# Second attention of a two-layer transformer kernel: values weighed in fp32 as two 64-column tiles, and the output projected inside the loop of head pairs

## What is computed

```python
xn = layernorm(x, ln_x_g, ln_x_b)              # the context, 77 rows
ln = layernorm(latents, ln_l_g, ln_l_b)        # the tokens, 1024 rows
q = heads(ln @ Wq)                             # 16 heads of 64
k, v = heads(concatenate([xn @ Wkv, ln @ Wkv]))
qn = rmsnorm(q, qn_g) * scale
kn = rmsnorm(k, kn_g)
attn = softmax(masked(qn @ kn.T))              # 1024 queries, 1024 + 77 keys
out = (attn @ v).reshape(1024, 16 * 64)
return out @ Wout + bout                       # added to the residual
```

## Time and profile before

| | us |
|---|---|
| median of 3 runs | 2465.91 |
| lowest and highest run | 2465.64, 2475.62 |
| profiled execution, span | 2477.3 |
| loop of pairs (736 to 1935 us of the span), PE busy | 1157.4 of 1199.0 |
| stage that projects the outputs (1942 to 2023 us), PE busy | 71.9 of 81.0 |

### The profile page before, as it was taken

The page is one execution under the profiler, slowest core; times in us unless marked ns, Lnnn a source line. Parts: engine busy times, 40 slices in busy tenths (PEclk is TensorE's granted clock), DMA queues, the critical chain, the costliest instruction groups (busy, mean ns, idle before and its releaser), DMA issues. The chain is left out here.

```text
span 2477.3 us, 40299 instructions
## 1 busy us (share of the span) xinstructions
PE 2096.9 (85%) x13062; PEld 1762.3 (71%) x13063; DVE 1409.2 (57%) x3260; ACT 1135.1 (46%) x2179; POOL 764.3 (31%) x733
## 2 busy tenths in 40 slices
PE   5889539997159999999999999999998863799994
PEld 3569535664149988899998898988898753466772
DVE  4370236664638777777778877778877314321223
ACT  3443202221127667666677766666766311222220
POOL 2100002332164443454444444434541000122220
PEclk9898759999569999999999999999999985899997
DMA  5421351111200000000000000000000347111113
GB/s 192 142 85 55 142 190 37 44 47 41 81 20 1 16 17 16 2 16 16 16 16 16 1 16 17 16 17 1 16 10 9 106 152 263 41 34 31 32 34 113
DMA packets 85352, 131.30 MB, mean 53 GB/s; under 512 B 9825, under 2 KB 70943, under 8 KB 83115
## 3 DMA queue, kind: packets, MB, share of 16 engines
q1 hardware_dynamic: 74539, 106.16, 12.6%
q0 software_dynamic: 8320, 20.65, 2.9%
q10 hardware_dynamic: 2304, 2.10, 0.2%
HBM read 87.89 MB, written 40.80 MB: 52 GB/s over the span
## 5 line engine op out<-in xcount | busy, mean ns | idle before, releaser
L1585 ACT ACTIVATE a_probT<-a_slot 128x512 fp32r<-128x512 f32 (+1 forms) x512 | 320.4, 651 | 345.6 <-PE a_slot L1480 343.5
L1639 DVE TENSOR_REDUCE a_part_peak<-a_slot 128x1 f32<-128x512 f32 (+1 forms) x512 | 354.6, 731 | 154.4 <-PE a_slot L1471 150.0
L1686 DVE TENSOR_TENSOR a_probT<-a_slot,a_probT 128x512 fp32r<-128x512 f32 (+1 forms) x512 | 369.6, 753 | 18.2 <-ACT a_probT L1585 15.6
L1471 PE MATMUL a_slot<-a_KHL,a_QHL 128*128 128x512 f32 (+1 forms) x1536 | 337.2, 355 | 20.9 <-DVE a_probT L1686 14.4
L1494 PE MATMUL a_po<-a_probT,a_VHL 128*128 128x256 f32 (+1 forms) x2322 | 339.9, 291 | 11.1 <-DVE a_O L1705 4.4
L1471 PEld LDWEIGHTS a_slot<-a_KHL,a_QHL 128*128 128x128 f32 x1536 | 271.9, 190 | 94.9 <-DVE a_probT L1686 37.9
L1494 PEld LDWEIGHTS a_po<-a_probT,a_VHL 128*128 128x128 f32 (+1 forms) x2322 | 293.2, 189 | 24.6 <-issue 24.6
L1480 PE MATMUL a_slot<-ident,a_prob 128*128 128x128 f32 x2048 | 282.9, 282 | 10.6 <-issue 10.2
L1577 ACT ACTIVATE a_prob<-a_slot,a_npeak 128x1024 f32<-128x1024 f32 x256 | 284.6, 1112 | 1.0 <-DVE a_npeak L1641 1.0
L1480 PEld LDWEIGHTS a_slot<-ident,a_prob 128*128 128x128 f32 x2048 | 221.7, 142 | 11.3 <-issue 10.7
L1420 PE MATMUL a_side<-a_W,a_latT 128*128 128x128 f32 x1536 | 194.7, 281 | 14.1 <-DMA a_W<-in_L_xattn_Wkv_dram 9.6
(11 more groups left out here) (331 smaller groups left out, 3411.3 us busy)
## 6 DMA issues: line engine op xcount, KB each, us to landing
m_up<-_L_ffn_gate_up_proj_dram SPq DMA_DIRECT2D x8, 1024.0 KB
a_o_rows<-a_O SPq DMA_DIRECT2D x16, 512.0 KB, 3.5
a1o_o<-a_o_rows SPq DMA_DIRECT2D x16, 512.0 KB, 3.5
m_up<-in_L_ffn_W_dram SPq DMA_DIRECT2D x8, 1024.0 KB
m_down<-in_L_ffn_W_dram SPq DMA_DIRECT2D x8, 1024.0 KB
a_prob_dram<-a0p_zeros SPq DMA_DIRECT2D x4, 1632.0 KB, 10.6
a_dist_dram<-a_dist SPq DMA_DIRECT2D x4, 1632.0 KB, 8.2
a_band_prob<-a_prob_dram SPq DMA_DIRECT2D x4, 1632.0 KB, 7.0
```

The lines of the kernel that those rows point to most:

```text
L1471: ins = t_.matmul(out[:, lo:hi], q, KHL[:, pair.parity, h, part, lo:hi], start=part == 0, stop=part == 1)
L1585: a_.activation(probT[:, u // 2 % 2, 0, lo:hi, u % 2, :], slot[u % 2][:, lo * P:hi * P].rearrange("p (t q) -> p t q", q=P), ACT.Copy).then ...
L1639: v.tensor_reduce(part[:, i:i + 1], slot[u % 2][:, lo:hi], AX.X, ALU.max).then_inc(part_peaked, 1)
L1686: v.tensor_tensor(pT[:, 1], slot[u % 2][:, lo * P:hi * P].rearrange("p (t q) -> p t q", q=P), pT[:, 0], ALU.subtract).then_inc(probT_low, 1)
```

## The change

- **Values and probabilities** are plain fp32, without a high and a low part. `V` holds 64 columns a head. `probT` is copied once: the first 4 tiles by ACT (`copy_first`), the other 5 by DVE (`copy_rest`), each as soon as its half is turned.
- **Groups** are four units: both heads, 256 queries. For each of the 9 key tiles `weigh` issues one fp32 matmul for each head, with 64 stationary columns and 256 moving ones: head 0 writes PSUM partitions 0 to 63, head 1 partitions 64 to 127. The 9 tiles are spread over four units as 2, 2, 2 and 3 (`PARTS`). `weigh` now stands ahead of `piece` in PE's order. `fold_outputs` is gone.
- **Sums**: `invert` also widens the inverses to 64 columns a head (`rwide`), PE transposes them into `side` (`turn_sums`, unit 2 of 4), ACT copies them (`copy_sums`), and `normalise` multiplies the transposed outputs by them (unit 0 of 4).
- **Output projection**: in unit 1 of 4, `project_outputs` multiplies the two 128-query tiles with the pair's 128 rows of `Wout` into `side` (two fp32 matmuls of 256 columns), and DVE adds all 512 columns to `xres` (`add_outputs`). `bout` is added to `xres` once, by POOL, after its first pair (`based`), and DVE waits for it ahead of its first unit. The later stage is gone, and so are the stores to HBM and the loads from it.
- `side` is now shared: PE waits for `added` and `r_out` ahead of the piece of such a unit, and for the copy of the piece before ahead of `project_outputs` and `turn_sums`.
- The three weight transfers of a pair are one, from an array laid out by pair on the host. Four memsets of POOL go. `all_pairs` writes out the first and the last pair and loops over the six between.

```diff
+PARTS = [[8, 0], [1, 2], [3, 4], [5, 6, 7]]
...
+def group_before(pair, u, by):
+
+    gi = u // 4 - by
+    return (pair, gi) if gi >= 0 else (pair.previous(), gi + GROUPS)
...
-        probT = sb("probT", [P, 2, 2, KT_TILES, 2, P], F32R)
+        probT = sb("probT", [P, 2, KT_TILES, 2, 2 * P])
...
+            pool.wait_ge(w_out_loaded, 32)
+            g_.tensor_tensor(xres[:, :, :], xres[:, :, :], bout[:, :].unsqueeze(1).to_broadcast([P, TILES, E]),
+                             ALU.add).then_inc(based, 1)
             body(Pair(1, 0, 0, 1), False)
...
                 if part == 0:
-                    pe.wait_ge(probT_low, (pair.g * GROUPS + gi) * 4 + 5)
-                    pe.wait_ge(o_out, pair.g * GROUPS + (gi + 2))
+                    pe.wait_ge(probT_act, pair.g * UNITS + (gi + 1) * 4)
+                    pe.wait_ge(probT_dve, pair.g * UNITS + (gi + 1) * 4)
+                    if gi or not (isinstance(pair.g, int) and pair.g == 0):
+                        pe.wait_ge(normalised, pair.g * GROUPS + gi)
                     if gi == 0:
-                        pe.wait_ge(dve_freed, count(pair, "Vb", SPLIT))
-                for j in range(KT_TILES):
+                        pe.wait_ge(act_freed, count(pair, "Vb", COPIED))
+                for j in PARTS[part]:
                     rows = P if j < S else CTX
-                    ins = t_.matmul(po_t, VHL[0:rows, pair.parity, j, gi % 2, :, :].rearrange("p a d -> p (a d)"),
-                                    probT[0:rows, gi % 2, part, j, :, :].rearrange("p t q -> p (t q)"),
-                                    start=part == 0 and j == 0, stop=part == 1 and j == S)
-                if part == 1:
+                    for h in range(2):
+                        ins = t_.matmul(po_t[h * D1:(h + 1) * D1, :], V[0:rows, pair.parity, j, h, :], probT[0:rows, gi % 2, j, h, :],
+                                        start=j == PARTS[0][0], stop=j == PARTS[-1][-1])
+                if part == len(PARTS) - 1:
                     ins.then_inc(weighed, 1)
 
-            def fold_outputs(pair, gi):
-
-                pe.wait_ge(OT_out, pair.g * GROUPS + (gi + 3))
-                for i in range(2):
-                    ins = t_.matmul(po_n[:, i * D1:(i + 1) * D1], OT[:, i * P:(i + 1) * P], fold[:, :], start=True, stop=True)
-                ins.then_inc(folded, 1)
+            def turn_sums(pair, gi):
+
+                pe.wait_ge(widened, pair.g * GROUPS + (gi + 1))
+                for t in range(2):
+                    ins = t_.transpose(side[:, t * P:(t + 1) * P],
+                                       rwide[:, t, :, :].rearrange("p h d -> p (h d)"), ident[:, :])
+                ins.then_inc(r_turned, 1)
+
+            def project_outputs(pair, gi):
+
+                pe.wait_ge(normalised, pair.g * GROUPS + (gi + 1))
+                for t in range(2):
+                    ins = t_.matmul(side[:, t * E:(t + 1) * E], OT[:, t * P:(t + 1) * P],
+                                    Wout[:, bass.ds(pair.hp, 1), :].rearrange("p a n -> p (a n)"), start=True, stop=True)
+                ins.then_inc(y_done, 1)
...
+                    one_before, two_before = group_before(pair, u, 1), group_before(pair, u, 2)
                     turn(pair, u)
-                    if u % 2 == 0:
-                        fold_outputs(*(pair, u // 2 - 2) if u >= 4 else (before, u // 2 - 2 + GROUPS))
+                    if u % 4 == 1 and two_before[0]:
+                        owner, gi = two_before
+                        if after:
+                            pe.wait_ge(act_freed if PIECES[u - 1] in COPIED else dve_freed,
+                                       count(after, PIECES[u - 1], COPIED if PIECES[u - 1] in COPIED else SPLIT))
+                        else:
+                            pe.wait_ge(r_out, owner.g * GROUPS + (gi + 1))
+                        project_outputs(owner, gi)
+                    if u % 4 == 2 and one_before[0]:
+                        owner, gi = one_before
+                        if after:
+                            pe.wait_ge(act_freed if PIECES[u - 1] in COPIED else dve_freed,
+                                       count(after, PIECES[u - 1], COPIED if PIECES[u - 1] in COPIED else SPLIT))
+                        elif two_before[0]:
+                            pe.wait_ge(added, owner.g * GROUPS + gi)
+                        turn_sums(owner, gi)
+                    if one_before[0]:
+                        weigh(*one_before, u % 4)
                     if after:
+                        if u % 4 == 1 and two_before[0]:
+                            pe.wait_ge(added, two_before[0].g * GROUPS + (two_before[1] + 1))
+                        if u % 4 == 2 and one_before[0]:
+                            pe.wait_ge(r_out, one_before[0].g * GROUPS + (one_before[1] + 1))
                         piece(after, PIECES[u])
-                    weigh(*(pair, u // 2 - 1) if u >= 2 else (before, GROUPS - 1), u % 2)
                     nxt = ahead(pair, u, 2)
                     if nxt[0]:
-                        pe.wait_ge(probT_low, (pair.g * UNITS + u) * 2 + 3)
+                        pe.wait_ge(probT_act, pair.g * UNITS + (u + 1))
+                        pe.wait_ge(probT_dve, pair.g * UNITS + (u + 1))
                         score(*nxt)
...
+            def copy_first(pair, u):
+
+                act.wait_ge(turned, (pair.g * UNITS + u) * 2 + 1)
+                t, h = tile_head(u)
+                a_.activation(probT[:, u // 4 % 2, 0:HALF, h, u % 2 * P:(u % 2 + 1) * P],
+                              slot[u % 2][:, 0:HALF * P].rearrange("p (t q) -> p t q", q=P), ACT.Copy).then_inc(probT_act, 1)
+
+            def copy_sums(pair, gi):
+
+                act.wait_ge(r_turned, pair.g * GROUPS + (gi + 1))
+                a_.activation(rT[:, :], side[:, 0:2 * P], ACT.Copy).then_inc(r_out, 1)
...
-                        copy_outputs(*(pair, u // 2 - 1) if u >= 2 else (before, GROUPS - 1))
...
+            def copy_rest(pair, u):
+
+                dve.wait_ge(turned, (pair.g * UNITS + u) * 2 + 2)
+                t, h = tile_head(u)
+                v.tensor_copy(probT[:, u // 4 % 2, HALF:KT_TILES, h, u % 2 * P:(u % 2 + 1) * P],
+                              slot[u % 2][:, HALF * P:KT_TILES * P].rearrange("p (t q) -> p t q", q=P)).then_inc(probT_dve, 1)
+
...
-                r = rsum[:, gi % 4, :]
-                dve.wait_ge(row_summed, (pair.g * GROUPS + gi) * 2 + 7)
-                v.reciprocal(r, r).then_inc(rsum_done, 1)
+                r = rsum[:, gi % 2, :, :]
+                dve.wait_ge(row_summed, (pair.g * GROUPS + (gi + 1)) * 4)
+                v.reciprocal(r, r).then_inc(inverted, 1)
+                dve.wait_ge(inverted, pair.g * GROUPS + (gi + 1))
+                v.tensor_copy(rwide[:, :, :, :], r.unsqueeze(3).to_broadcast([P, 2, 2, D1])).then_inc(widened, 1)
 
             def normalise(pair, gi):
 
-                n = pair.g * GROUPS + (gi + 3)
-                r = rsum[:, gi % 4, :]
-                dve.wait_ge(rsum_done, n)
-                dve.wait_ge(folded, n)
-                if gi == 0:
-
-                    dve.wait_ge(o_stored[pair.parity], (pair.g - pair.parity) * 8 + 16)
-                t, h = tile_head(2 * gi)
-                v.tensor_tensor(O[:, pair.parity, t:t + 2, h * D1:(h + 1) * D1], po_n.rearrange("p (t d) -> p t d", t=2),
-                                r.unsqueeze(2).to_broadcast([P, 2, D1]), ALU.mult).then_inc(o_out, 1)
+                dve.wait_ge(r_out, pair.g * GROUPS + (gi + 1))
+                dve.wait_ge(weighed, pair.g * GROUPS + (gi + 1))
+                v.tensor_tensor(OT[:, :], po_t, rT[:, :], ALU.mult).then_inc(normalised, 1)
+
+            def add_outputs(pair, gi):
+
+                dve.wait_ge(y_done, pair.g * GROUPS + (gi + 1))
+                tile = pair.b * S + 2 * gi
+                x = xres[:, tile:tile + 2, :].rearrange("p t e -> p (t e)")
+                v.tensor_tensor(x, x, side[:, :], ALU.add).then_inc(added, 1)
...
-                    if u % 2 == 0:
-                        normalise(*(pair, u // 2 - 2) if u >= 4 else (before, u // 2 - 2 + GROUPS))
-                    copy_low(pair, u, 0)
-                    copy_low(pair, u, 1)
+                    two_before = group_before(pair, u, 2)
+                    if u % 4 == 0 and two_before[0]:
+                        normalise(*two_before)
+                    copy_rest(pair, u)
+                    if u % 4 == 1 and two_before[0]:
+                        add_outputs(*two_before)
                     row_sum(pair, u)
-                    if u % 2:
-                        invert(*(pair, u // 2 - 1) if u >= 2 else (before, GROUPS - 1))
+                    if u % 4 == 3:
+                        invert(pair, u // 4)
...
-        with ExitStack() as c3:
...
```

More of the change, by code:

```diff
@@ L1364, in body @@
                     tiles = nat.shape[1]
-                    if j == 0:
-                        pool.wait_ge(high, count(pair, step, SPLIT))
```

(44 more changed lines are left out.)

169 lines of the change are left out of this document (38 added, 131 removed).

## The result

| | before | after |
|---|---|---|
| median of 4 runs each, us | 2466.82 | 2485.56 |
| lowest and highest run, us | 2465.64, 2475.62 | 2483.53, 2486.92 |
| profiled execution, span, us | 2477.3 | 2481.7 |
| from the first turn to the end of the phase, us | 735.59 to 2022.20: 1286.6 | 724.38 to 2026.78: 1302.4 |
| plain pair (median, from one piece c to the next), us | 74.3 | 80.5 |

The ratio is 1.0064, with a 95% interval of 1.0045 to 1.0083: the change makes the kernel slower, by 16 us by the ratio. The phase that was changed is 15.8 us longer. The forecast was 2455, a ratio of 0.996, so it has the wrong sign; 2485.6 lies inside its range.

A forecast was written before the change was run, and what follows sets the result against it. PE was taken to bound the loop of pairs. Stage -80, 15 pairs +67, last pair -8, tail +4, start +7, loads -1 sum to -11 us on the median of 2465.9: 2455, range 2390 to 2560.

The forecast's parts named there:

- The stage, -80: Behind the loop: the 80.2 us stage with its 16 loads and 16 stores, all on the path, goes; -80 us.
- Copies: DVE and ACT in the loop: one plain copy each stays of two passes; the score's wait for the copies falls away.
- part 4: One pair in the loop with its new waits: 78.6 us against 74.1, +4.5 a pair, +67 over 15 pairs.
- The price of weigh (part 3): PE's new weigh: two head halves overlap but start in program order; 1.08 us for two key tiles, 1.51 for three.
- the rival's 0.86 and 1.30: Faster rival: the heads' passes in weigh interleave wholly, 3.4 us less a pair, 55 in all: 2400 us; chance 0.20.
- the array is emptied at each change of tile shape: Slower rival: weigh's two shape changes cost 0.32 us a unit, 5.1 a pair, 82 in all: 2537 us; chance 0.16.
- The sum of a pair: PE's loop: projection units 37.4, K pieces 25.4, Q pieces 15.8; 78.6 us a pair against 74.1, +4.5.
- The five K units: Units whose K piece stands behind weigh, so the next turn waits for exponentials: together 25.4 us, against 19.9 of PE's own work.
- the two that count: New PE waits: unit 0 of 4's weigh for normalise (starts at 1.64, not 1.04 us); turns after K pieces for exponentials.
- The form of the loop changes, not its number of turns: 0: The loop over pairs: its rewritten form was priced at 0, since the number of turns stays.
- Start, +7: Start of the phase: DVE's first copy waits 6 us for POOL's bias addition, and PE cools; +7, between 0 and 10.
- "likeliest" case of 0.47: The forecast case, 2455 us, halves overlapping in program order: chance 0.47, own range 2435 to 2478.

The follow-up runs named there:

- experiment 7: Kernel after, with weigh's records issued head by head within a part and not alternating by key tile: 2522.86 us, ratio 1.0205 to the kernel before.
- experiment 11: Kernel after, with each weigh record taking both heads' values as one 128-column tile, so no 64-column tiles: 2669.30 us, ratio 1.0797 to the kernel before.
- experiments 1, 2 and 4: Kernel after, reordered: pieces ahead of weigh in two units of four, 2425.19 us; normalise ahead of the maximum, 2455.04; every piece ahead of weigh and more, 2392.76.
- experiment 8: Kernel before, with weigh issued ahead of the piece in every unit and nothing else changed: 2585.10 us, ratio 1.0458 to the kernel before.
- experiment 2: Kernel after, with DVE normalising at the end of unit 3 of 4, ahead of the maximum: 2455.04 us, ratio 0.9936 to the kernel before.
- experiment 9: Fully reordered kernel (every piece ahead of weigh), with POOL adding the bias ahead of its first pair: 2383.26 us, ratio 0.9651 to the kernel before.
- experiment 3: Kernel after, with DVE's wait for the bias moved to ahead of its first addition to the residual: 2489.34 us, ratio 1.0076 to the kernel before.

## Why the prediction was wrong, point by point

**The stage, -80**: right; nothing takes its place.

**Copies**: right. The wait of the earlier trace rows is gone, and the exponentials and `normalise` are late next, as part 4 said.

**The price of weigh (part 3)**: the step that failed, in two halves. "The halves ... run at once but start in program order", 1.08 and 1.51: in fact they interleave wholly, since PE reaches past a waiting record (experiment 7). At the rival's 0.86 and 1.30 that gives back 3.4 a pair. Against it the other rival, "the array is emptied at each change of tile shape", priced at 5.1 a pair, has its price too: the change of shape costs 4.3 (experiment 11), and the gap that I had named as its sign, from the last record of a weigh to the piece, is 0.31 and not 0.22. I had put them as alternatives to the forecast, at 0.20 and 0.16. They hold together, and no case of mine had both. Inside weigh they nearly cancel, so that 1.02 and 1.44 stand against my 1.08 and 1.51: that is luck. What the sum lacked is the part of the price that falls on the work ahead of weigh and behind it. (Trainium skill, TensorEngine Tiling (Array Packing), Key Properties: tiles run loads and matmuls in parallel, and switching mode needs a drain. The runs agree with the first, 0.42 us for four records on two tiles, and the gap of 0.31 fits the second.)

**The sum of a pair**: forecast +4.5, measured 80.5 - 74.3 = +6.2. Of the 78.6 forecast, -3.4 + 4.3 gives 79.5. For the other 1.0 the rows show a score behind a piece at 1.15 where I took 1.10, in the 11 units where PE's own work sets the pace (some 0.6). One pair, from the turn at 1285.16 to that at 1365.82 us, takes 80.66, and by the terms of part 4 its 2.1 over the forecast are, in those 11 units: weigh itself -0.68; the work ahead of it +0.80 (`project_outputs` 0.96 and not 0.86, a turn 1.13 and not 1.04); the pieces behind it +0.84 (1.81 and not 1.70, 0.41 and not 0.36); the score +0.58; the wait for `normalise` +0.33 (weigh 1.84 and 1.77 behind its turn and not 1.64); and in the K units +0.20. The first three, which the change of shape and the interleaving make, come to +0.96 a pair: over 15 pairs 14 of the 27 us between the -11 forecast and the +16 measured. The five K units were right: forecast 25.4, measured 5.23 + 4.99 + 5.67 + 5.02 + 4.64 = 25.6 (units 7 to 11). Their waits and that for `normalise`, which I called the two that count, do count: experiments 1, 2 and 4 take them away for 92 us, and experiment 8 puts them into the old kernel.

**"The form of the loop changes, not its number of turns: 0"**: the number is the same, four, but a pair with the branch is 4.7 longer than a plain one in the kernel before (79.0 on average) and 5.7 in the kernel after (86.2), and that is 4 us. The wait for `normalise` behind the idle time of the branch has its part in it: without it the four are 2.3 longer than a plain pair (experiment 2). The falling clock is not new, though: it fell in the kernel before as well (0.52 from 889.30 to 892.00 us, behind an idle of 2.61), and in the kernel after one turn at the branch already took 1.96 ahead of that wait (at 1626.18 us).

**Start, +7**: right in size (experiment 9 takes 7 off) and half right in cause. Had the semaphore not been there, DVE's row sum would have stood beside POOL's addition instead (experiment 3). **Tail**: 12.1 forecast, 12.2 measured. **Last pair**: -8 forecast, -6 measured. **Loads**: -1 forecast; PE waited 9.6 for them as before, so 0.

**The sum**: from the first turn to the last pair's first turn the kernel after takes 97.5 us more, start included, where I had 67 + 7; then -6, +4 and -80: +16 by the profile, as by the ratio, where I had -11. "I am wrong if a pair takes under 76 or over 81": it takes 80.5, within the band, but the bound of 81 stood 2.4 x 15 = 36 us above a forecast that was only 11 below zero. The number that decided the sign was the least certain one, and 15 pairs multiply it. The split of the chances, 0.41 to 0.39, said as much; that a "likeliest" case of 0.47 rested on a middle value of the weigh that no row showed was its weakness.

The cause is settled as far as order goes: the same work in another order is 3 to 3.5% faster than before. What stays open is why a score behind a piece takes 1.15, how the 4 us at the branch divide between waits and clock, and how far PE reaches past a waiting record.

## What to carry to other kernels

Work moved into a loop that one engine bounds costs its own length only if it stands where nobody waits for what is behind it: put first what another engine needs next (here the piece, before the exponentials), and the work nobody waits for last. A block that covered a wait has a worth that its length doesn't show, so price a reordering with the work it covered. When two rivals don't exclude each other, work out the case in which both hold.

## What the runs showed of the hardware

- Two 64-column tiles on opposite halves of the array run at once: 0.42 us for four fp32 records of 256 moving columns, against 0.43 for two such records when they share the columns. They may be issued four records apart; at six the overlap is lost in part.
- Going over to 64 columns and back costs some 0.27 us for both changes together, from two kernels whose weighs are serial. The next work starts 0.31 us behind the last 64-column record, against 0.22 where the shape stays.
- A row sum on DVE with two SBUF inputs took 7.40 us in place of 0.29 beside a POOL addition of 8.87 us; a copy out of PSUM beside the same addition took its usual 0.82. A later semaphore wait cured nothing; moving POOL's work did.
- After PE had idled 1.97 us and, with one turn between, 1.75 more, the granted clock stood at its lower level (0.50 from 1140 to 1143 us), and a weigh and a piece took 2.4 us longer (1.90 + 3.28 between starts, against 1.02 + 1.80). After an idle of 1.63 us at the same branch with none behind it they took their usual time. One idle can be enough: behind 1.92 us a turn took 1.96 at 1626.18 us and its usual 1.09 at 969.59 us, and in the kernel before one took 1.96 behind 2.61.
